# Second attention of a two-layer gated block: scores on stacked high and low parts, queries and keys one step ahead, division by the sums behind the values

## The reference, cut to what matters

```python
b, s1, _ = x.shape
k_dca = _ln(kv_dca[:, :, 0], kn_dca_w, kn_dca_b)      # 16 special keys
q = _ln((x @ Wq + bq).reshape(b, s1, H, HD), qn_w, qn_b)
k = _ln(kv[..., :HD], kn_w, kn_b)                      # 240 plain keys
ctx     = _attn(qT, k.transpose(0, 2, 1, 3), v.transpose(0, 2, 1, 3))
ctx_dca = _attn(qT, k_dca.transpose(0, 2, 1, 3), v_dca.transpose(0, 2, 1, 3))
ctx = ctx + DCA_WEIGHT * ctx_dca
return ctx @ Wo + bo
```

## Time and profile before

| | |
|---|---|
| three runs | 3547.07, 3542.10, 3546.26 us; median 3546.26 us |
| the profiled execution | 3546.12 us, of which the span is 3544.4 us |
| busy share of the span | PE 98%, PEld 85%, DVE 65%, ACT 53%, POOL 38% |
| granted PE clock, mean | 0.989 |
| chain that ended last | PE 19% of the span, all of it in the lines of the last part |
| second attention | steps run from about 2195 to 2849 us of the span |

### The profile page before, as it was taken

The page is one execution under the profiler, slowest core; times in us unless marked ns, Lnnn a source line. Parts: engine busy times, 40 slices in busy tenths (PEclk is TensorE's granted clock), DMA queues, the critical chain, the costliest instruction groups (busy, mean ns, idle before and its releaser), DMA issues. The chain is left out here.

```text
span 3544.4 us, 66282 instructions
## 1 busy us (share of the span) xinstructions
PE 3464.4 (98%) x22490; PEld 3000.9 (85%) x22490; DVE 2313.4 (65%) x5703; ACT 1866.7 (53%) x4822; POOL 1339.6 (38%) x1345
## 2 busy tenths in 40 slices
PE   9999999999999999899999998899999989999999
PEld 8999999999999999799999996667777668888887
DVE  6666666656666666576767778787777754545543
ACT  5555555554444444455555554787777743333332
POOL 3222222332333322254544554777777640202020
PEclk9999999999999999899999999999999999999999
DMA  4566666535666665577767764222222245344341
GB/s 166 188 237 236 236 238 237 167 98 189 236 236 233 230 235 167 184 272 251 261 250 261 259 247 143 68 89 67 64 70 64 73 128 160 110 129 126 112 131 48
DMA packets 430862, 611.00 MB, mean 172 GB/s; under 512 B 95120, under 2 KB 226320, under 8 KB 426512
## 3 DMA queue, kind: packets, MB, share of 16 engines
q1 hardware_dynamic: 330128, 394.91, 34.1%
q10 hardware_dynamic: 90208, 179.32, 13.7%
q0 software_dynamic: 10272, 33.63, 2.8%
...
## 5 line engine op out<-in xcount | busy, mean ns | idle before, releaser
L853 POOL TENSOR_TENSOR a_prob<-a_prob,a_rinv 128x512 f32<-128x512 f32 x256 | 266.4, 1041 | 1005.2 <-DVE a_rinv L1071 1005.2
L773 ACT ACTIVATE a_prob<-a_prob,a_low_bias 128x256 f32<-128x256 f32 x512 | 256.5, 502 | 469.7 <-DVE a_low_bias L1062 468.2
L527 PE MATMUL a_pj<-a_xt,in_hi 128*128 128x256 f32 x1024 | 309.8, 302 | 0.1
L1378 POOL TENSOR_TENSOR e_act_hi<-e_act_f,e_zeros 128x256 fp32r<-128x256 f32 x128 | 181.5, 1418 | 308.0 <-DVE e_act_f L1608 308.0
L1392 PE MATMUL e_gb<-e_xt_hi,in_hi 128*128 128x256 f32 x1024 | 291.7, 285 | 1.4 <-DVE e_xt_lo L1587 1.4
L1393 PE MATMUL e_gb<-e_xt_lo,in_hi 128*128 128x256 f32 x1024 | 290.9, 284 | 0.0
L1394 PE MATMUL e_gb<-e_xt_hi,in_lo 128*128 128x256 f32 x1024 | 290.9, 284 | 0.0
L2997 DVE TENSOR_TENSOR raw_in<-turned,raw_in 128x512 f32<-128x512 f32 x224 | 151.9, 690 | 212.5 <-PE turned L2710 209.6
L529 PE MATMUL a_pj<-a_xt,in_lo 128*128 128x256 f32 x1024 | 289.0, 282 | 0.0
L528 PE MATMUL a_pj<-a_xt,in_hi 128*128 128x256 f32 x1024 | 288.8, 282 | 0.0
L901 DVE TENSOR_TENSOR a_ot_lo<-a_avb,a_ot_hi 128x256 fp32r<-128x256 f32 x256 | 108.4, 423 | 258.2 <-ACT a_ot_hi L782 258.0
...
## 6 DMA issues: line engine op xcount, KB each, us to landing
...
```

The lines of the kernel that those rows point to most:

```text
L527: nc.tensor.matmul(out, a_hi, b_hi, start=start, stop=False)
L773: e = nc.scalar.activation(prob[:, u % 4, t], prob[:, u % 4, t], ACT.Exp, bias=low_bias[:, u % 2, t:t + 1], scale=-1.0, accum_out=rsum[:, ...
L853: nc.gpsimd.tensor_tensor(prob[:, u % 4], prob[:, u % 4], rinv[:, u % 2].unsqueeze(2).to_broadcast([P, 2, S]), ALU.mult).then_inc(p_done, 1)
```

## The change

- **Scores.** ACT writes queries and keys in float32 into `parts[0]` and `parts[3]` and their rounded high parts into `parts[1]`, `parts[2]` (a view of a former bias tile). POOL makes the low parts in place (`low_parts`). SP writes three combinations to DRAM (`qk_parts`) and reads them back so that high and low parts of one head stand under each other in 96 partitions of `stack` (`stack_heads`: three writes and three reads of 256 KB per group). `scores` is then four products over 128 partitions in the reduced type in place of four float32 products over 32.
- **Division.** POOL no longer multiplies the 480 plain columns; it multiplies only the 64 special ones, by the ratio of the two sums, and makes that ratio in an instruction of its own. Behind `values` PE spreads the reciprocals over `avb[:, S:]` with 8 small float32 products, ACT copies them out (`inv_f`), DVE multiplies in the following odd step (`scale_out`), and POOL splits the result into `ot_hi` and `ot_lo` (`split_out`).
- **Moved.** The squares go from the head of ACT's step to the end of POOL's. Everything from the gathering to the transposed queries and keys stands one step earlier. In odd steps PE does the transposes of queries and keys first and the early unit after the first transpose of probabilities; o1 is wholly late. The reciprocal waits for `values` of two groups before.

Work that stands in each step of a batch's period, after the change: step 0: `qk` of group 2, q1 (12 products); step 1: none; step 2: `qk` 3, v1 (6); step 3: v0 (6); step 4: o0 (12); step 5: `qk` 0, k0 (6), o1 (12); step 6: `qk` 1, k1 (6), transposes of x; step 7: q0 (12). `values` stands in each even step.

```diff
-        qk = sb("qk", [P, 2, 2 * S])
+        stack = sb("stack", [P, 2, 2, 2 * S], F32R)
+        parts = bd_sb.rearrange("p n d -> p (n d)").rearrange("p (k s) -> p k s", s=S)
...
-        for n, a, b in ((-10, ("k0", 0), None), (-9, ("k1", 0), None), (-8, ("q0", 0), ("q0", 1)), (-7, ("q1", 0), ("q1", 1)), (-6, None, ("v1", 0)),
-                        (-5, ("v0", 0), None), (12, ("o0", 0), ("o0", 1)), (13, ("o1", 0), ("o1", 1))):
+            plan(n - 18, "gather", n)
+        for n, a, b in ((-11, ("k0", 0), None), (-10, ("k1", 0), None), (-9, None, ("q0", 0)), (-9, None, ("q0", 1)), (-8, ("q1", 0), ("q1", 1)), (-6, None, ("v1", 0)),
+                        (-5, ("v0", 0), None), (12, ("o0", 0), ("o0", 1)), (13, None, ("o1", 0)), (13, None, ("o1", 1))):
             if a:
                 plan(n, "early", *a)
             if b:
                 plan(n, "late", *b)
-        plan(-9, "turn")
-        for n, k in ((-9, "k0"), (-7, "q0"), (-6, "q1"), (-5, "v1"), (-4, "v0"), (13, "o0"), (14, "o1")):
+        plan(-10, "turn")
+        for n, k in ((-10, "k0"), (-8, "q0"), (-7, "q1"), (-5, "v1"), (-4, "v0"), (13, "o0"), (14, "o1")):
             plan(n, "take", k)
-        plan(-9, "take_late", "k1")
-        plan(-9, "stats")
-        plan(-8, "root")
-        plan(-8, "square", 1)
-        plan(-6, "square", 0)
-        plan(-7, "hsum", 1)
-        plan(-5, "hsum", 0)
-        plan(-5, "head", 0)
+        plan(-10, "take_late", "k1")
+        plan(-10, "stats")
+        plan(-9, "root")
+        plan(-9, "square", 1)
+        plan(-7, "square", 0)
+        plan(-8, "hsum", 1)
+        plan(-6, "hsum", 0)
+        plan(-6, "head", 0)
         for g in range(GROUPS):
-            plan(2 * g - 4 if g else -3, "scale", g)
-            plan(2 * g - 3 if g else -2, "qk", g)
+            plan(2 * g - 5 if g else -4, "scale", g)
+            plan(2 * g - 4 if g else -3, "qk", g)
...
-        FIRST, AHEAD, LAST = -13, PAIRS, B * PAIRS + 15
+        FIRST, AHEAD, LAST = -14, PAIRS, B * PAIRS + 15
...
+            def stack_heads(b, g):
+                N = GROUPS * b + g
+                rows = qk_parts[N % 2]
+                sp.wait_ge(parts_hid, N + 1)
+                for r, cols in enumerate((slice(1, 3), slice(1, 4, 2), slice(0, 3, 2))):
+                    if r == 1:
+                        sp.wait_ge(parts_done, N + 1)
+                    sp.dma_start(rows[r].rearrange("p (k s) -> p k s", k=2), parts[:, cols]).then_inc(parts_kept[r > 0], 16)
+                if N:
+                    sp.wait_ge(s_ready, 2 * N)
+                for r in range(3):
+                    if r < 2:
+                        sp.wait_ge(parts_kept[r], (16, 32)[r] * (N + 1))
+                    sp.dma_start(stack[r * HD:(r + 1) * HD].bitcast(F32).rearrange("p n j c -> p (n j) c"), rows[r].rearrange("(j p) c -> p j c", p=HD)).then_inc(stacked, 16)
...
             def scores(i, n):
-                g, first = divmod(n, 2)
-                if first == 0:
-                    pe.wait_ge(taken["qk"], 2 * GROUPS * i + g + 1)
+                if n % 2 == 0:
+                    pe.wait_ge(stacked, STACK * PAIRS * i + STACK * (n // 2) + STACK)
                 pe.wait_ge(e_done, LOOP * i + n + 1)
                 for t in range(2):
                     for j in range(2):
-                        at = (2 * first + j) * HD
-                        mm = nc.tensor.matmul(sc[:, n % 2, j, t * S:(t + 1) * S], qk[at:at + HD, g % 2, t * P:(t + 1) * P],
-                                              qk[at:at + HD, g % 2, S:], start=True, stop=True)
+                        mm = nc.tensor.matmul(sc[:, n % 2, j, t * S:(t + 1) * S], stack[:, n % 2, j, t * P:(t + 1) * P], stack[:, n % 2, j, S:], start=True, stop=True)
                 mm.then_inc(s_ready, 1)
 
             def turn_p(i, n, j):
                 head = 2 * (LOOP * i + n) + j
-                pe.wait_ge(p_done, head + 1)
+                if j == 0:
+                    pe.wait_ge(p_done, LOOP * i + n + 1)
                 pe.wait_ge(pt_done, head + 1)
...
-                pe.wait_ge(ot_lod, group + 1)
+                pe.wait_ge(ot_done, group + 1)
                 if at == 0:
                     pe.wait_ge(taken["v0"], 2 * i + bb + 1)
                     pe.wait_ge(taken["v1"], 2 * i + bb + 1)
                 for k in range(2):
                     for j in range(HG):
                         h = at * HG + j
-                        mm = nc.tensor.matmul(avb[j * HD:(j + 1) * HD, 0:S], v[:, bb % 2, k, h * HD:(h + 1) * HD], pt[:, g % 2, j, k], start=k == 0, stop=k == 1)
+                        nc.tensor.matmul(avb[j * HD:(j + 1) * HD, 0:S], v[:, bb % 2, k, h * HD:(h + 1) * HD], pt[:, g % 2, j, k], start=k == 0, stop=k == 1)
+                first = 2 * (g % 2)
+                for t in range(2):
+                    for j in range(HG):
+                        at = 2 * (j % 2) + t
+                        mm = nc.tensor.matmul(avb[j * HD:(j + 1) * HD, S + t * P:S + (t + 1) * P], rinv[:, first + j // 2, 1, at:at + 1].to_broadcast([P, HD]), ident[:], start=True, stop=True)
                 mm.then_inc(av_ready, 1)
...
                 if u % 2:
-                    early()
+                    turned_qk()
                     if past == 0:
                         turn_ahead(0)
...
                 if u % 2:
-                    turned_qk()
+                    early()
                     if pair(i, u + 1):
                         scores(i, u + 1)
...
-                        l = nc.scalar.activation(qk[:, g % 2, cols], of[:, cols], ACT.Identity, bias=ln_sb[:, 2 * n + 1:2 * n + 2], scale=ln_sb[:, 2 * n:2 * n + 1])
+                    of, N = room(f"qk{g}"), GROUPS * (2 * i + bb) + g
+                    if not isinstance(i, int) or N:
+                        for n in range(2):
+                            act.wait_ge(parts_kept[n], (16, 32)[n] * N)
+                    else:
+                        act.wait_ge(dca_taken, 4)
+                    for n, (to, cols) in enumerate(((parts[:, 0], slice(0, S)), (parts[:, 3, 0:DCA], slice(S, S + DCA)), (parts[:, 3, DCA:], slice(S + DCA, 2 * S)))):
+                        l = nc.scalar.activation(to, of[:, cols], ACT.Identity, bias=ln_sb[:, 2 * n + 1:2 * n + 2], scale=ln_sb[:, 2 * n:2 * n + 1])
                     l.then_inc(taken["qk"], 1)
+                    act.wait_ge(taken["qk"], N + 1)
+                    nc.scalar.copy(parts[:, 1:3].bitcast(F32R), parts[:, 0:4:3]).then_inc(parts_hid, 1)
 
             def step(i, u):
-                if u == -4:
+                if u == -5:
                     act.wait_ge(ln_scaled, 1)
-                for bb, half in due(i, u, "square"):
-                    b = 2 * i + bb
-                    act.wait_ge(taken["k1" if half else "q1"], b + 1)
-                    act.wait_ge(hsum_done, 2 * b + 2 - half)
-                    nc.scalar.activation(sq[:], nrm[:, bb % 2, 2 * half:2 * half + 2], ACT.Square).then_inc(sq_done, 1)
                 if pair(i, u):
                     exps(i, u, 0)
+                queries_and_keys(i, u)
                 if u % 2 == 0:
-                    queries_and_keys(i, u)
                     if pair(i, u - 2):
                         copy_pt(i, u - 2, 0)
-                    if pair(i, u - 4):
-                        g = (u - 4) // 2
-                        act.wait_ge(av_ready, 2 * GROUPS * i + g + 1)
-                        nc.scalar.copy(ot_hi[:, g // GROUPS % 2, g % GROUPS], avb[:, 0:S]).then_inc(ot_hid, 1)
                     if pair(i, u):
                         exps(i, u, 1)
...
+                if u % 2 == 0:
+                    if pair(i, u - 4):
+                        g = (u - 4) // 2
+                        act.wait_ge(av_ready, 2 * GROUPS * i + g + 1)
+                        if pair(i, u - 6):
+                            act.wait_ge(ot_lod, 2 * GROUPS * i + g)
+                        nc.scalar.copy(inv_f[:], avb[:, S:]).then_inc(inv_done, 1)
...
+            def split_out(i, g):
+                N = 2 * GROUPS * i + g
+                hi, lo = (w[:, g // GROUPS % 2, g % GROUPS] for w in (ot_hi, ot_lo))
+                pool.wait_ge(ot_done, N + 2)
+                T(hi, ot_f[:], zeros[:], ALU.add).then_inc(ot_hid, 1)
+                pool.wait_ge(ot_hid, N + 1)
+                T(lo, ot_f[:], hi.bitcast(F32), ALU.subtract).then_inc(ot_lod, 1)
+
+            def low_parts(i, bb, g):
+                pool.wait_ge(parts_hid, GROUPS * (2 * i + bb) + g + 1)
+                T(parts[:, 0:4:3].bitcast(F32R), parts[:, 0:4:3], parts[:, 1:3], ALU.subtract).then_inc(parts_done, 1)
...
                     n = u - 1
                     pool.wait_ge(r_done, LOOP * i + n + 1)
-                    p, r = prob[:, n % 4], rinv[:, n % 4]
-                    T(p[:, :, :, 0:DCA], p[:, :, :, 0:DCA], r[:, 0].rearrange("p (h t) -> p h t", h=2).unsqueeze(3).to_broadcast([P, 2, 2, DCA]), ALU.mult)
-                    for j in range(2):
```

(25 more changed lines are left out.)

73 lines of the change are left out of this document (46 added, 27 removed).

## The result

The changed kernel takes 3638.57 us (median of four runs, 3630.95 to 3644.26) against 3545.78 of the kernel before: ratio 1.0262, 95% interval 1.0241 to 1.0283, +93 us. The forecast was 3661 in a range of 3590 to 3740. The profiled run took 3637.42 us, span 3635.6. Of the 91 us that the span grew, 76 lie between the first and the last maxima of this part (730.2 us against 654.5); the first maxima come 10 us later (2204.55 against 2194.51), and some 5 are at the end.

A forecast was written before the change was run, and what follows sets the result against it. PE was taken to bound plain batches, a second limit 4% under. Afterwards stretches of 21 + 28 = 49 us replace 41.54, 7.5 more; 16 x 7.5 = 120, less 5, is +115: 3546 to 3661 us, range 3590 to 3740.

The forecast's parts named there:

- signs of being wrong: Batches under 42 us; POOL waiting long for reciprocals in steps 0 and 1; scores waiting for `stack`; clock under 1.00.
- Stretch A: From pair 6's reciprocal (step 7) to pair 1's (step 2): POOL and DVE run in turn, 15.84 to 21 us.
- Stretch B: From pair 1's reciprocal to pair 6's: late DVE and PE's waits make 25.69 into 28 us, 2.4 more.
- Two takes and a hand-over, 1.6: Step 6: group 1's transposes wait 1.6 us for room that DVE empties behind o1.
- links of 0.68: Three DVE instructions of 0.68 us each, in the 8.5 us of DVE work up to `scale_out` in step 3.
- Had ACT kept the squares: Claim that with squares on ACT (1.07 us each) DVE would not wait ahead of pair 1's reciprocal.
- PE's own gain: Cheaper scores save 4.6 us per batch, reciprocal spreads cost 2.4: at most 2.2 us gained per batch.
- DMAs at nothing: Transfers of parts through DRAM costed at zero: 14 us needed, scores that need them 15 to 17 us away.
- Rival 2: Transfers come late, once write and read together pass 9 us; 3 us more gives 3709 us; chance 0.06.
- Rival 3: The clock falls as PE idles; mean clock 0.9 adds 4 us per batch, 3700 us; chance 0.06.
- Rival 1: Only the order costs, POOL is cheap: +3 us per batch, 3592 us; chance 0.13.
- 1.76 per split: POOL's splits at 1.76 us if contending with DVE, making the sum some 60 us higher; low values were taken.

The follow-up runs named there:

- run 1: The changed kernel with its squares back on ACT, at the head of its step: 3635.53 us, ratio 1.0264.
- run 5: The kernel before with only the change's timetable; scores, division and squares as before: 3647.29 us, ratio 1.0302.
- run 2: The kernel before with only its squares moved from ACT to the end of POOL's step: 3631.81 us, ratio 1.0257.
- run 6: The kernel before with the change's timetable, but half of q1's products moved from step 0 into empty step 1: 3610.03 us, ratio 1.0184.
- run 11: The kernel before with cheap scores alone, reduced precision summed over four heads (results left wrong): 3504.81 us, ratio 0.9899.
- run 3: The changed kernel without the DRAM transfers, scores waiting for the low parts instead: 3613.04 us, ratio 1.0208.
- run 4: The changed kernel with POOL's squares, low parts and splits shrunk to 16 columns, waits and order kept: 3603.64 us, ratio 1.0182.

## Why the prediction was right, and where its reasons were not

- **Sign and size.** +93 us where +115 was forecast, inside the range. That it is so near is in part luck: a plain batch lost 4.3 us at full clock (45.8) and 4.6 on average where 7.5 were put, only the made ones lost the 7.5 (7.2 and 8.2 in the two above), and 15 us more came ahead of the first maxima and behind the last, where the forecast had 5 less. Of its own signs of being wrong two came: scores that wait for `stack`, and a clock under 1.00 inside the part.
- **Stretch A: 21 forecast, 20.3 measured.** The chain is the one described: squares, DVE's sum, reciprocal, POOL. Squares took 1.89 us, not 2.40 (both operands are the same tile here, L861 reads two; whether that is the reason was not tried); splits 0.74 and low parts 1.27, as taken; the ratio 0.35 on average for 0.21. POOL is at 32.1 us per batch, where 34 was forecast. DVE's waits for the squares are 5.3 us per batch, where 8 were put.
- **Stretch B: 28 forecast, 25.6 measured, no loss.** This is the mis-sized term. "Two takes and a hand-over, 1.6" for group 1's transposes is an error of order: these use the bank that k0 had, and DVE takes k0 (2700.87) ahead of o1 (2702.45), so the transposes at 2703.16 wait for nothing. And the links of 0.68 went to 0.27 (below): `scale_out` of step 3 starts 5.4 us after the reciprocal of pair 1 (2683.96 to 2689.37), where 8.5 were put (its terms add to 8.8). Waits for copies out of `ptb` took part of that back, and `values` starts at 7.4. From there PE's work takes 10.9 us (to 2702.24) where 11.1 were put, and the rest 7.3 where 8.5 were put.
- **The step that failed is the cause given for A.** "Had ACT kept the squares, DVE would not wait here" is true, and worth nothing (run 1). The prediction counted the change's instructions, and took the timetable as the place where they meet; it never put down PE's products step by step (12, 0, 6, 6, 12, 18, 6, 12) as a cost of its own. In the old kernel the timetable alone costs 106 us (run 5) and the squares alone 93 (run 2); the change has both, with cheaper scores and less work for POOL, and costs 93. So they do not add up there, and the record counts of run 1 fit that PE works off its surplus of products while POOL's squares hold up the probabilities. No run has the two and nothing else, so this is argued and not shown. Of the timetable's 106 us, 42 hang on the hole in step 1, most of them by the clock (run 6). Of what is left, 49 us are more idle time of PE (78.4 against 29.5), 3.9 us in a plain batch and spread over four waits (run 6), none of which was taken away alone; a candidate is step 5, 7.62 us between reciprocals in the changed kernel with PE busy 7.42, against 3.47.
- **PE's own gain.** Four scores take 0.55 from start to start (2724.84 to 2725.39), the spread costs 0.55, and the values 0.89 (2691.35 to 2692.24) for 1.00 from start to start before; PE's busy time in a plain batch at full clock went from 41.19 to 38.78, 2.4 us, where 2.2 were put. Even alone, in the old timetable, cheap scores bring 36 us (run 11).
- **DMAs at nothing.** Off by 19 to 25 us (run 3): scores wait 23.7 us for `stack` in the part, and the start is some 8 us later. Rival 2 was a part of the truth, not a case of its own.
- **The clock.** Rival 3 came in part. In the changed kernel six of the nine plain batches are at 1.00, but the others and the made ones are at 0.89 to 0.96, and the mean from the first to the last maxima is 0.95 (0.97 before), where the rival had 0.9. By these two means the lower level lasted about 73 us of 730 in place of 39 of 654. An estimate from this: 34 us more at half rate are some 17 us of work, of the 76 that this part lost. In runs 2 and 5 it came in full, with means of 0.92 and 0.91 and 35.8 and 46.5 us more busy time of PE. Why the changed kernel has less of it than run 5 was not tested.
- **Rival 1** (only the order costs, POOL is cheap) put 46 us on a kernel with cheap squares. Run 4 is nearly that kernel and still costs 1.8%, 64 us, but it has A at 15.9 and B at 27.7, and by its length its loss does not lie in POOL's busy time.
- **POOL beside DVE.** By the rule of the "GPSIMD Engine Reference" in the Trainium skill (section Specifications) GpSimd contends with VectorE instructions that have two SBUF inputs, and the prediction drew 1.76 per split from it. The splits took 0.74 and 0.73 on average over 63, but that does not speak against the rule: only five of the 126 met such an instruction of DVE. In one of them DVE had started first (L2502 `raw_in<-raw_in,raw_out` at 2235.00, the split at 2235.41), and the split took 1.18. In four the split had started first and kept 0.73 or 0.74, and DVE's L2504 `d_v<-d_v,raw_out` took 0.90 to 0.92 (as at 2270.95). The trace agrees with the rule.
